# An R-GCN layer on one core: SyncE fetches five groups of rows instead of two, from byte addresses, into two sets of places

## The reference

```
h = relu(layernorm(x))
out = h @ W_root + bias
for r in range(8):
    m   = (edge_type == r)
    agg = segment_sum((h[src] @ W[r]) * m, dst)
    cnt = segment_sum(m, dst)
    out = out + agg / maximum(cnt, 1)
return x + out
```

## Time and profile before

| | |
|---|---|
| time, median of 3 runs | 1247.79 us (1245.68 to 1250.12) |
| the profiled execution: span from first to last instruction | 1020.0 us |
| the profiled execution's own time | not listed in the page; the median less the span is 227.8 us, which lies around the span |
| PE busy | 769.5 us (75%), 4342 matmuls |
| POOL busy | 757.4 us (74%), 808 instructions |
| DVE busy | 706.0 us (69%) |
| ACT busy | 413.9 us (41%) |
| indirect gathers from the table on POOL | 771, mean 950 ns |
| DMAs of one row on SP | 768, 0.5 KB each |

### The profile page before, as it was taken

One profiled execution on the slowest core, in us unless ns is written; L12 is line 12 of the kernel. 1 busy time (PEld: TensorE's weight loads), 2 busy tenths in 40 slices (PEclk: granted clock), 3 DMA queues, 4 the chain that ended last, 5 costly groups with the idle time before them and its releaser, 6 DMA issues.

```text
span 1020.0 us, 17379 instructions
## 1 busy us (share of the span) xinstructions
PE 769.5 (75%) x4342; PEld 634.1 (62%) x4342; DVE 706.0 (69%) x2309; ACT 413.9 (41%) x821; POOL 757.4 (74%) x808
## 2 busy tenths in 40 slices
PE   0488786887888777877877868878778687787787
PEld 0277675675666665655756756657657566675676
DVE  7798978768776767576666566665765756657676
ACT  7985253352343342432432423423424334243242
POOL 7677777777777777777777777777777777777772
PEclk9996767667676776676676676676766867667679
DMA  9694222222222222222222222222222222222221
GB/s 275 185 226 92 55 58 55 57 57 55 57 56 58 58 58 58 55 59 58 57 56 58 58 55 60 56 58 59 55 59 57 56 60 56 57 58 56 59 57 29
DMA packets 53978, 71.57 MB, mean 70 GB/s; under 512 B 15523, under 2 KB 39110, under 8 KB 53878
## 3 DMA queue, kind: packets, MB, share of 16 engines
q0 software_dynamic: 25440, 52.15, 20.2%
q1 hardware_dynamic: 28438, 18.30, 7.0%
HBM read 63.99 MB, written 6.40 MB: 69 GB/s over the span
## 4 chain that ended last, share of the span: by engine, by line
POOL 52%; issue 19%; PE 14%; DVE 6%; DMA 4%; ACT 4%; SPq 1%; DVEq 0%; POOLq 0%
POOL hg L540 52%; PE acc L1560 5%; PE fin L1591 4%; DMA hg<-h_table,src_i 4%; PE zp L1580 1%; ACT h_all L611 1%; DVE x_all L1146 1%; PE zp L1598 1%; DVE onehot L1048 1%; ACT hg L639 1%; PE acc L1567 1%; PE acc L1564 1%; DMA x_all<-in_x 1%; PE zp L1597 1%; DVE ring L1062 1%
## 5 line engine op out<-in xcount | busy, mean ns | idle before, releaser
L540 POOL DMA_INDIRECT hg<-h_table,src_i x771 | 732.6, 950 | 237.2 <-issue 229.2
L1560 PE MATMUL acc<-onehot,hg 128*128 128x96 f32 (+1 forms) x1602 | 408.3, 367 | 200.7 <-DMA hg<-h_table,src_i 168.4
L1560 PEld LDWEIGHTS acc<-onehot,hg 128*128 128x128 f32 x1602 | 320.9, 249 | 278.6 <-issue 207.1
L1062 DVE TENSOR_TENSOR ring<-ring,acc 128x512 f32 x267 | 181.8, 681 | 239.2 <-PE acc L1567 229.5
L663 ACT ACTIVATE hT<-zp 128x116 f32<-128x116 f32 x50 | 13.4, 267 | 516.3 <-PE zp L1598 516.0
L1048 DVE TENSOR_SCALAR onehot<-iota,key_f 128x96 f32<-128x96 f32 (+1 forms) x801 | 197.2, 293 | 11.4 <-issue 2.6
L1564 PE MATMUL acc<-onehot,ones_bf 128*128 128x96 bf16 (+1 forms) x801 | 204.0, 255 | 0.0
L1591 PE MATMUL fin<-w_sb,blk 128*116 128x128 f32 x800 | 179.3, 398 | 0.0
L1591 PEld LDWEIGHTS fin<-w_sb,blk 128*116 128x116 f32 x800 | 161.6, 288 | 11.9 <-issue 11.7
L653 ACT ACTIVATE loop_far<-iota,loop_key 96x256 f32<-96x256 f32 x267 | 134.0, 502 | 40.9 <-PE acc L1567 28.7
L1146 DVE SCALAR_TENSOR_TENSOR x_all<-fin,inv,x_all 116x128 f32<-116x128 f32 x400 | 139.1, 348 | 14.4 <-DVE x_all L1136 0.5
(11 more groups left out here) (152 smaller groups left out, 369.1 us busy)
## 6 DMA issues: line engine op xcount, KB each, us to landing
hg<-h_table,src_i POOLq DMA_INDIRECT x771, 2.5
hg<-h_table SPq DMA_DIRECT2D x768, 0.5 KB
out<-x_all SPq DMA_DIRECT2D x53, 58.0 KB
x_all<-in_x SPq DMA_DIRECT2D x7, 384.0 KB, 7.9
h_table<-h_all SPq DMA_DIRECT2D x7, 384.0 KB
h_all<-h_table SPq DMA_DIRECT2D x5, 504.0 KB
x_all<-in_x SPq DMA_DIRECT2D x5, 504.0 KB
w_sb<-in_L_gnn_W SPq DMA_DIRECT2D x1, 512.0 KB
```

What stands on the lines that cost most here:

```text
L540: nc.gpsimd.indirect_dma_start(out=hg[:, slot_of(t), :], out_offset=None, in_=x if g < XG else table, in_offset=bass.IndirectOffsetOnAxis( ...
L1062: nc.vector.tensor_tensor(ring[:, :, :, at], ring[:, :, :, at], acc[:, q, :, :].rearrange("p a (r n) -> p a r n", r=R), ALU.add).then_inc( ...
L1560: nc.tensor.matmul(both[:, 0, :, a:e], hg[:, slot, :], hot.rearrange("p (r n) -> p r n", r=R), start=(j == 0), stop=(j == n - 1), skip_gro ...
```

## The change

- SP fetches five groups (84, 129, 173, 217, 264) instead of two. They go into two sets of three tile places in turn (`FETCH_SETS = 2`), so the number of places stays six. Before the third and every later group SP waits until the group before it in the same set is summed.
- The fetching is spread over the stores of blocks 3 to 47.
- DVE multiplies the source numbers of a fetched group by 512, the bytes of a row, into `late_bytes` (`late_addresses`, called right behind `split_words` of the part that holds the group), which raises `late_ready`. SP copies the 384 addresses of a group at once (`fetch_addresses`, five copies instead of six) into `late_words` and uses each as a byte offset into the table, seen as bytes.
- `fetch_addresses` for the next group is called behind the first batch of 16 rows of the current one, as before for the next tile.
- The rows of a group are fetched in the order partition by partition, the three tiles in turn.
- `e_rows` is no longer an array of its own: it is `e_rows_i` seen as float32, and the edge data are converted in place.
- The semaphore `top_made` is folded into `eps_made`.

```diff
-FETCHED = (209, 264)
+FETCHED = (84, 129, 173, 217, 264)
+FETCH_SETS = 2
 FETCH = 16
-FETCH_FROM = 7
-FETCH_TO = 46
+FETCH_FROM = 3
+FETCH_TO = 48
...
-        e_rows = sb("e_rows", [RC, 3, CHUNKS, RAW + 1])
+        e_rows = e_rows_i[:, :, :, :].bitcast(f32)
...
             if t // GT in FETCHED:
-                return 2 * IT + fetched_tiles().index(t)
+                return 2 * IT + FETCHED.index(t // GT) % FETCH_SETS * GT + t % GT
...
-            def fetch_sources(k):
-
-                part = max(n for n, first in enumerate(PART_GROUPS) if first <= late[k] // GT)
-                sp.wait_ge(src_ready, part + 1)
-                sp.dma_start(late_src[:, k % 2 * P:(k % 2 + 1) * P], src_i[:, late[k]:late[k] + 1]).then_inc(late_src_in, 16)
+            def fetch_addresses(k):
+
+                sp.wait_ge(late_ready, k + 1)
+                sp.dma_start(late_at[:, k % 2, :, :], late_bytes[:, k * GT:(k + 1) * GT]).then_inc(late_src_in, 16)
 
             def fetch_rows(c):
 
-                k, at = divmod(c * FETCH, P)
+                k, at = divmod(c * FETCH, GT * P)
                 regs = [sp.alloc_register(f"late{c}_{n}") for n in range(FETCH)]
-                sp.wait_ge(late_src_in, 16 * (k + 1))
-                sp.load(regs, late_src[0:1, k % 2 * P + at:k % 2 * P + at + FETCH])
+                if at == 0:
+                    sp.wait_ge(late_src_in, 16 * (k + 1))
+                    if k >= FETCH_SETS:
+                        sp.wait_ge(group_summed, FETCHED[k - FETCH_SETS] + 1)
+                sp.load(regs, late_row[:, k % 2 * GT * P + at:k % 2 * GT * P + at + FETCH])
                 for n in range(FETCH):
-                    row = sp.snap(regs[n], donate=True, min_val=0, max_val=N - 1)
-                    sp.dma_start(hg[at + n:at + n + 1, slot_of(late[k]), :], table[bass.ds(row, 1), :]).then_inc(
-                        fetched[k // GT], 16)
-                if at == 0 and k + 1 < len(late):
-                    fetch_sources(k + 1)
+                    p, j = divmod(at + n, GT)
+                    row = sp.snap(regs[n], donate=True, min_val=0, max_val=(N - 1) * ROW_BYTES)
+                    to = slot_of(FETCHED[k] * GT + j) * ROW_BYTES
+                    sp.dma_start(hg_bytes[p:p + 1, to:to + ROW_BYTES],
+                                 table_bytes[bass.ds(row, ROW_BYTES)].rearrange("(a f) -> a f", a=1)).then_inc(
+                        fetched[k % FETCH_SETS], 16)
+                if at == 0 and k + 1 < len(FETCHED):
+                    fetch_addresses(k + 1)
...
+            def late_addresses(part):
+
+                first, end = PART_GROUPS[part], (PART_GROUPS + [GALL])[part + 1]
+                for k, g in enumerate(FETCHED):
+                    if first <= g < end:
+                        dve.wait_ge(src_ready, part + 1)
+                        nc.vector.tensor_scalar(late_bytes[:, k * GT:(k + 1) * GT], src_i[:, g * GT:(g + 1) * GT], ROW_BYTES,
+                                                None, ALU.mult).then_inc(late_ready, 1)
...
                         split_words(part_at(i, q, 3, 3))
+                        late_addresses(part_at(i, q, 3, 3))
```

More of the change, by code:

```diff
@@ L60, in start_of @@
     return t * P if t <= WHOLE else WHOLE * P + (t - WHOLE) * RAW
-def fetched_tiles():
-    return [g * GT + j for g in FETCHED for j in range(GT)]
 def window(j):
@@ L93 @@
 NODE_BITS = 13
+ROW_BYTES = 4 * F
 NOWHERE = 1023
@@ L112, in rgcn @@
 def rgcn(nc, x, src, dst, etype, w, w_root, bias, out):
-    f32, bf16, i32 = mybir.dt.float32, mybir.dt.bfloat16, mybir.dt.int32
+    f32, bf16, i32, u8 = mybir.dt.float32, mybir.dt.bfloat16, mybir.dt.int32, mybir.dt.uint8
     ALU, ACT, AX = mybir.AluOpType, mybir.ActivationFunctionType, mybir.AxisListType
@@ L168, in rgcn @@
         key_f = sb("key_f", [P, CHUNKS * RC])
+        late_words = sb("late_words", [1, 2 * GT * P], i32)
+        late_bytes = sb("late_bytes", [P, len(FETCHED) * GT], i32)
         loop_key = sb("loop_key", [GT * SLOTS, CHUNKS * RG])
@@ L173, in rgcn @@
         at_i = sb("at_i", [1, ITERS, PLACES], i32)
-        hg = sb("hg", [P, 2 * IT + len(FETCHED) * GT, F])
+        hg = sb("hg", [P, 2 * IT + FETCH_SETS * GT, F])
         onehot = sb("onehot", [P, IT, OHW])
@@ L229, in rgcn @@
         g_c = hg_flat[:, R * VW + 5 * P + 2 * VW:R * VW + 5 * P + 2 * VW + R]
-        late_src = e_rows_i[:, :, :, :].rearrange("p a c w -> p (a c w)")[0:1, 0:2 * P]
+        late_row = late_words[:, :]
+        late_at = late_row.rearrange("a (k p j) -> a k p j", k=2, j=GT)
         g_h = hg_flat[:, R * VW + 5 * P + VW:R * VW + 5 * P + 2 * VW]
@@ L250, in rgcn @@
         pads, ident_made, iota_made = sem("pads"), sem("ident_made"), sem("iota_made")
-        eps_made, ones_made, zeros_made, ring_cleared, top_made = (
-            sem("eps_made"), sem("ones_made"), sem("zeros_made"), sem("ring_cleared"), sem("top_made"))
+        eps_made, ones_made, zeros_made, ring_cleared = sem("eps_made"), sem("ones_made"), sem("zeros_made"), sem("ring_cleared")
         table_loaded = sem("table_loaded")
@@ L272, in rgcn @@
         gathered = [sem(f"gathered{j}") for j in range(2 * IT)]
-        fetched = [sem(f"fetched{g}") for g in FETCHED]
-        late_src_in = sem("late_src_in")
+        fetched = [sem(f"fetched{k}") for k in range(FETCH_SETS)]
+        late_src_in, late_ready = sem("late_src_in"), sem("late_ready")
         group_summed, group_added = sem("group_summed"), sem("group_added")
@@ L437, in store @@
                              x_all[0:n, bass.ds(b, 1), :].rearrange("p a f -> p (a f)")).then_inc(stored, 16)
-            late = fetched_tiles()
-            def fetch_sources(k):
-                part = max(n for n, first in enumerate(PART_GROUPS) if first <= late[k] // GT)
-                sp.wait_ge(src_ready, part + 1)
-                sp.dma_start(late_src[:, k % 2 * P:(k % 2 + 1) * P], src_i[:, late[k]:late[k] + 1]).then_inc(late_src_in, 16)
+            hg_bytes = hg[:, :, :].rearrange("p s f -> p (s f)").bitcast(u8)
@@ L461, in _ @@
+                if at == 0 and k + 1 < len(FETCHED):
+                    fetch_addresses(k + 1)
+            batches = len(FETCHED) * GT * P // FETCH
             done = 0
@@ L464, in _ @@
                 if b == FETCH_FROM:
-                    fetch_sources(0)
+                    fetch_addresses(0)
                 while done < min(batches, batches * (b + 1 - FETCH_FROM) // (FETCH_TO - FETCH_FROM)):
@@ L965, in extremes @@
                     checked(nc.vector.tensor_reduce(ext[0:RC, k * len(PARTS) + part:k * len(PARTS) + part + 1], v[:, 0:n, :], AX.XY, op))
-            nc.vector.memset(top[:, :, :], 0.0).then_inc(top_made, 1)
+            nc.vector.memset(top[:, :, :], 0.0).then_inc(eps_made, 1)
             for k in range(NORM_STEPS):
@@ L982, in _ @@
                                     ALU.add).then_inc(src_conv, 1)
-            dve.wait_ge(top_made, 1)
+            dve.wait_ge(eps_made, 3)
             nc.vector.memset(ext[:, :], 0.0).then_inc(check_step, 1)
@@ L1557, in sums_of @@
                     elif j == 0:
-                        pe.wait_ge(fetched[FETCHED.index(g)], 16 * GT * P)
+                        pe.wait_ge(fetched[FETCHED.index(g) % FETCH_SETS], 16 * GT * P * (FETCHED.index(g) // FETCH_SETS + 1))
                     nc.tensor.matmul(both[:, 0, :, a:e], hg[:, slot, :], hot.rearrange("p (r n) -> p r n", r=R),
```

2 lines of the change are left out of this document (1 added, 1 removed).

## The result

The changed kernel takes 1534.5 us (median of 5 runs, 1533.3 to 1538.57); the kernel before took 1247.0 us beside it (5 runs, 1245.68 to 1250.12). The ratio is 1.231, 95% interval 1.2296 to 1.2325. The sign was forecast, and the mechanism in outline; the forecast size, 1285 us, lies far off.

A forecast was written before the change was run, and what follows sets the result against it. POOL's gathers were taken to bound the kernel, SP's fetching to bound it after the change. Group 264 lands at 1038.3, plus 16.8 and 1.5 gives span 1056.6; plus 227.8 gives 1284.4, forecast 1285 us, 3% slower; range 1250 to 1330 us.

The forecast's parts named there:

- the slack of the earlier trace: SP's queue waited 505 us for blocks to store, so SP was no bound; the change would use this up.
- SP becomes the bound, five stalls of PE: SP never idles after 211 us; PE waits some tens of us before each of the five fetched groups.
- The instructions of a row: On SP: byte addresses remove FUSED_REGOPS, MOVE stays with the DMA; 0.075 us saved, 0.339 us per row.
- The price of a batch, 6.8 us: SP's time for 16 rows with their register load falls from 8.0 to 6.8 us; 120 batches take 816 us.
- My upper bound of 8.0 us: SP's batch if byte addresses save nothing: 143 us more than the forecast, 1428 us.
- The new wait: SP stands from about 152 to 211 us for group 129's addresses, with one batch of 120 done.
- The end: Behind group 264's arrival: 16.8 us for the last groups and block, plus 1.5 us for a lower PE clock.
- Around the span: Median of the runs 1247.79 us less the profiled span 1020.0: 227.8 us outside the span, left unchanged.
- The gain on offer, 11.2 us: POOL does 9 gathers less at 1.25 us each, ending 11.2 us earlier if the fetched rows arrive in time.
- The small edits at 0: Five DVE multiplications, conversion in place and the folded semaphore: taken at 0, with 1.5 us either way.
- The rule weighed against the trace: Skill page: small transfers descriptor-bound, 0.68 us each; 1920 rows 1306 us, span past 1300; rejected for the trace's 0.41 us pitch.
- rows dearer: Rival: SP's batch stays at 8.0 us, 1428 us, or 1356 us if the DMA takes 40 ns more; chance 0.13.

The follow-up runs named there:

- b0_before_again: The kernel before, unaltered, run and traced once more: 1232.69 us, ratio 1.0001, span 1230.5 us.
- e3_late_call: The changed kernel with the call for the next group's addresses moved behind the last batch of a group: 1485.15 us, ratio 1.204 to the kernel before.
- e1_no_rows: The kernel before with no group fetched on SP, POOL gathering all: 1227.81 us, ratio 0.997 to the kernel before.
- e10b_left_out: The changed kernel with its five groups neither fetched nor gathered, PE multiplying zeros: 1013.02 us, ratio 0.9894 to the kernel before, 1023.78 us on that chip.
- e9_no_rows_in_place: The changed kernel with no group fetched on SP, keeping the in-place conversion and folded semaphore: 1226.97 us, ratio 0.9958 to the kernel before.
- e5_fixed_rows: The changed kernel with its 1920 row DMAs at constant addresses, without register loads and MOVEs: 1233.84 us, ratio 1.0009 to the kernel before.
- e2_bytes_two_groups: The changed kernel with only the two old groups (209, 264) and the old pauses: 1237.15 us, ratio 1.0034 to the kernel before.
- e4_row_numbers: The changed kernel with SP again multiplying row numbers by 512, one more instruction per row: 1726.92 us, ratio 1.4034 to the kernel before.
- e8_ticks: The kernel before without fetched rows, plus 3825 increments of an unused semaphore on SP: 1244.25 us, ratio 1.0104 to the kernel before.
- f1_after_again: The changed kernel, unaltered, run again on a fifth chip: 1532.01 us, ratio 1.2304 to the kernel before, 1245.17 us there.

## Why the prediction was right about the sign and wrong about the size

The forecast span was 1056.6 us, the measured one 1532.4. The step that failed is the price of a batch on SP: 6.8 us were forecast, and beside POOL's gathers it is 11.9. With it fell the slack of the earlier trace rows: in the timed executions SP had none to give. Term by term:

- **SP becomes the bound, five stalls of PE**: right. Five waits for rows, SP never waiting for blocks, POOL out of the chain and waiting behind PE in long pieces.
- **The instructions of a row**: right. FUSED_REGOPS gone, MOVE stays; the medians are unchanged, and where POOL does not gather a batch costs what was forecast (48 rows with their loads in 18.39 us, 0.38 each, and 6.8 / 16 = 0.42 in the forecast, which holds the pauses too).
- **The price of a batch, 6.8 us**: this is the mis-sized term. From the address copy at 289.85 to the last row at 1512.6 are 1222.8 us; less 14.1 for stores and 2 for copies and landing, as in the prediction's sum, that is 1206.7 / 119 = 10.14 us, where 11.9 us beside gathers and 6.6 without are mixed. 119 x 3.34 = **397 us**. My upper bound of 8.0 us came from the same trace and so could not hold it.
- **The new wait**: right in place and kind; but the addresses came at 289.85 and not at 211 us, **79 us** later, because the start of the kernel is longer too at this pace (SP's first row of before starts at 303.4 us in `b0_before_again` and at 224.3 in the earlier trace rows). Its worth, against a call that does not wait, is some 33 us (`e3_late_call`).
- **The end**: right. 16.8 + 1.5 = 18.3 us forecast behind the arrival of group 264; from 1513.93 to the end of the span are 18.5. A first matmul takes 0.71 us there, against 0.36 in the earlier trace rows.
- **Around the span**: 227.8 us forecast, 2.1 measured (1534.5 - 1532.4). **-226 us.** I took a difference between two different kinds of execution for time outside the program, as the table ahead of the prediction does, and no row showed any work there.
- The sum: 1284.4 + 397 + 79 - 226 = 1534, the measured time. It has to come out, since the 10.14 us are taken from the measured end; the batches measured by themselves (77 x 11.9 + 43 x 6.6) say the same within 2%. The errors are of opposite sign and have one cause, the pace of the timed executions; that they partly cancel is luck, and against the forecast change of 37 us the measured one is 287.5.
- **The gain on offer, 11.2 us**: absent on the chips of the comparison (`e1_no_rows`: six gathers more, and no slower), measured as 10.8 us on the chip with the pace of the trace (`e10b_left_out`). The reading of POOL as the bound fits the execution shown, and that was not the execution timed.
- **The small edits at 0**: right for the conversion in place and the semaphore (`e9_no_rows_in_place`); the multiplications were not tested by themselves.
- **The rule weighed against the trace**: the Trainium skill ("DMA: Bandwidth & Descriptors", section "Measured (HBM→SBUF, 128 partitions, SWDGE, issued from GpSimd)") would have made the rows themselves the cost; `e5_fixed_rows` issues all 1920 for 0.09% and the interval holds zero. It did not bear on this case, though the time by it, over 1300 us, an estimate from that page, lay nearer to the result. The same page of the Trainium skill ("Issuing engines are not separate DMA queues") says that issuing from another engine saves only the sequencer's issue time, "which is usually small relative to the DMA itself". Here the time that SP takes to issue is the price: 512 bytes a DMA, and the loss is gone when SP has fewer instructions for the same DMAs (`e5_fixed_rows`).

Of the rivals, "rows dearer" came nearest, and named the wrong reason (elements of one byte, a serial queue): `e5_fixed_rows` has the same DMAs and no loss of its kind, and the median of a DMA is 228 ns as before.

How it all fits: beside POOL's gathers SP gets through about three instructions per us, and of which kind they are matters little. It is 2.75 in `b0_before_again` (49 in 17.8 us), 2.8 in `e2_bytes_two_groups` (33 in 11.7), 3.1 in `e4_row_numbers` (49 in 16.0), 2.7 in `e5_fixed_rows` (16 DMAs in 5.9) and 3.3 in `e8_ticks`. Without gathers it depends on the kind: 5.0 in the changed kernel (33 in 6.6), 6.3 in `e4_row_numbers`, 15 in `e8_ticks`. The kernel before asks for 48 x 49 in 39 pauses of 22.4 us, 2.7 per us, just what there is; three groups for 72 x 33 in 41 pauses, 2.6; `e5_fixed_rows` for 1.9; the changed kernel for 120 x 33 in 45, **3.9**. Of these only the last does not fit, and the excess waits for stalls of PE. In them POOL stops gathering too, and SP doubles its pace.

## What to carry to other kernels

Compare the traced span with the timed runs before anything else is read: here 1020 against 1247 us said that the trace was of another kind of execution, and that every gap and every wait in it could be off, above all the slack of the engine that gets the new work. An engine that only issues has a budget of instructions per us, and on the chips of the comparison it shrank beside POOL's gathers: count all instructions (address arithmetic and register moves too) against the pause that they must fit in. When a list of waits says how idle an engine is, check it against the engine's own gaps. Where a fetch hides nothing that bounds, leave it out: at this pace both kernels are slower than the one without any, the kernel before by 0.3%.

## What the runs showed of the hardware

- **Two paces.** The same program takes 1023.8 us on one chip and 1232 to 1249 on five, steady within 0.4% on each but for one execution. The gathers' own duration is the same (median 0.944 and 0.947 us), the gaps differ. It is not SP's load: without any row it takes 1227.8.
- **TensorE's clock** does not explain the pace as far as one execution can say. Beside `f1_after_again` one execution of the kernel before had a mean granted clock of 1.0, the upper of the two levels, where its neighbours had 0.64 to 0.67, and took 1275.8 us, more than their 1245. It was not repeated, and something else may have differed in it.
- **At the slow pace SP's instructions are stretched in steps while POOL gathers.** Of the increments in `e8_ticks` half take 17 ns or less and others some 700 or 1400; the longest MOVE is 42 ns in the earlier trace rows, 773 in `b0_before_again` and 1394 after. With the last gather the steps are gone, though PE, DVE and ACT run on (x533 at 17/17/17 ns). It needs no DMA of SP. On the chip of the trace the same gathers (161 in 200 us) leave SP's instructions clean.
- **A full SP slows the others a little**: PE's last sum is at 1231.0 us with 1920 rows that nobody waits for and at 1230.1 with bare increments, against 1215.3 with neither.
- **Open** is what POOL's gathers and SP share (that the steps go with the gathers is read from the traces, no run takes the gathers away with the rest running; POOL's issuing and the transfers of its gathers were not told apart; the supply of instructions or the writing of records would be candidates), whether the same thing makes the gaps of PE, DVE and ACT, why one chip lacks it, and whether the changed kernel would there cost the 3% that its trace promised.
